# The opening of an adapter-and-mix kernel: first block of columns in two halves, two issuing queues, block 0 normalised first

## The reference

```python
# x: (8 samples, 1024 rows, 512), one row id of L0 and one of L1 per sample
w1, w2 = W1[ids0], W2[ids0]                     # 512x128 and 128x512 per sample
h = relu(x @ w1 + b1[ids0])
r = x + h @ w2 + b2[ids0]
n = (r - mean(r)) * rsqrt(var(r) + 1e-5) * gamma[ids0] + beta[ids0]
x1 = x + n
out = x1 + x1 @ W[ids1] + b[ids1]               # 512x512 per sample
```

## Time and profile before

| | |
|---|---|
| median of 3 runs | 309.87 us (309.72 to 310.06) |
| the profiled execution | 310.4 us, its span 308.6 us |
| TensorE busy | 301.1 us (98%) |
| VectorE, GpSimd, ScalarE busy | 225.7, 225.7, 212.0 us |
| granted TensorE clock | 1.00 throughout |
| moved by DMA | 65.13 MB, mean 211 GB/s |

### The profile page before, as it was taken

One profiled execution on the slowest core, in us unless ns is written; L12 is line 12 of the kernel. 1 busy time (PEld: TensorE's weight loads), 2 busy tenths in 40 slices (PEclk: granted clock), 3 DMA queues, 4 the chain that ended last, 5 costly groups with the idle time before them and its releaser, 6 DMA issues.

```text
span 308.6 us, 4770 instructions
## 1 busy us (share of the span) xinstructions
PE 301.1 (98%) x1406; PEld 242.4 (79%) x1406; DVE 225.7 (73%) x643; ACT 212.0 (69%) x382; POOL 225.7 (73%) x185
## 2 busy tenths in 40 slices
PE   8789999999999999999999999999999999999995
PEld 6335788888888888888888888888888888888884
DVE  0089968886969879596887969688795968889610
ACT  1139778885887859686696858968596874867431
POOL 0299966999599995999779995999959994631000
PEclk9999999999999999999999999999999999999999
DMA  6999994879766896878866897668867371111122
GB/s 184 331 374 365 363 288 162 226 229 324 227 165 190 254 271 198 221 206 250 261 172 209 218 314 244 133 194 264 292 183 208 133 276 34 70 68 70 70 102 102
DMA packets 40817, 65.13 MB, mean 211 GB/s; under 512 B 6101, under 2 KB 10197, under 8 KB 40790
## 3 DMA queue, kind: packets, MB, share of 16 engines
q1 hardware_dynamic: 40498, 64.29, 67.8%
q10 hardware_dynamic: 292, 0.52, 0.5%
HBM read 48.03 MB, written 16.78 MB: 210 GB/s over the span
## 4 chain that ended last, share of the span: by engine, by line
PE 90%; DVE 3%; DMA 2%; SPq 2%; issue 1%; POOL 0%; ACT 0%; DVEq 0%
PE out_ps L814 56%; PE down_ps L814 13%; PE h_ps L814 13%; PE turn_ps L876 9%; DMA xrow<-x_rows 2%; DVE y L520 1%; SPq L177 1%; DVE stats L525 1%; SPq L186 1%; DVE turn_ps L564 0%; DVE x1T_lo L571 0%; POOL xrow L723 0%; PE out_ps L876 0%; ACT out_sb L423 0%; SPq L209 0%
## 5 line engine op out<-in xcount | busy, mean ns | idle before, releaser
L814 PE MATMUL out_ps<-x1T_hi,w_hi 128*128 128x512 f32 x256 | 100.0, 391 | 0.0
L814 PE MATMUL out_ps<-x1T_hi,w_lo 128*128 128x512 f32 x256 | 99.7, 389 | 0.0
L723 POOL TENSOR_TENSOR xrow<-xrow,b_rows 128x512 f32<-128x512 f32 x64 | 82.3, 1292 | 11.9 <-DMA xrow<-x_rows 11.7
L814 PE MATMUL out_ps<-x1T_lo,w_hi 128*128 128x512 f32 x256 | 68.6, 390 | 0.0
L414 ACT ACTIVATE x1T_hi<-turn_ps,gamma_beta 128x512 fp32r<-128x512 f32 x62 | 41.9, 690 | 37.7 <-DVE turn_ps L564 37.7
L564 DVE SCALAR_TENSOR_TENSOR turn_ps<-turn_ps,gamma_beta,xT 128x512 f32<-128x512 f32 x62 | 44.0, 752 | 32.4 <-PE turn_ps L876 31.7
L405 ACT ACTIVATE y<-y,shift,rstd 128x512 f32<-128x512 f32 x64 | 52.0, 817 | 22.0 <-DVE shift L555 21.7
L728 POOL TENSOR_TENSOR xT_lo<-xT,xT_hi 128x512 fp32r<-128x512 f32 x48 | 62.2, 1296 | 1.5 <-ACT xT_hi L354 1.5
L520 DVE TENSOR_TENSOR y<-down_ps,xrow 128x512 f32<-128x512 f32 x64 | 43.7, 684 | 19.8 <-PE down_ps L814 18.8
L814 PEld LDWEIGHTS out_ps<-x1T_hi,w_hi 128*128 128x128 f32 x256 | 48.1, 188 | 10.2 <-ACT x1T_hi L414 0.2
L814 PEld LDWEIGHTS out_ps<-x1T_hi,w_lo 128*128 128x128 f32 x256 | 48.1, 188 | 9.9
(11 more groups left out here) (50 smaller groups left out, 359.6 us busy)
## 6 DMA issues: line engine op xcount, KB each, us to landing
out_cols<-out_sb SPq DMA_DIRECT2D x64, 256.0 KB, 2.8
xrow<-x_rows SPq DMA_DIRECT2D x30, 512.0 KB, 6.7
xT<-x_cols SPq DMA_DIRECT2D x28, 512.0 KB, 6.1
w<-w_all SPq DMA_DIRECT2D x8, 1024.0 KB, 7.6
w<-w_all SPq DMA_DIRECT2D x16, 256.0 KB, 5.2
b_rows<-b_all SPq DMA_DIRECT2D x7, 256.0 KB, 8.8
xT<-x_cols SPq DMA_DIRECT2D x6, 256.0 KB, 6.0
xrow<-x_rows SPq DMA_DIRECT2D x4, 256.0 KB, 6.7
```

The costliest lines, as they stand in the source:

```text
L723: nc.gpsimd.tensor_tensor(xrow[:, i % XR, :], xrow[:, i % XR, :], b2_rows[:, m % 2, :], ALU.add).then_inc(rowbias_done, 1)
L814: mm = nc.tensor.matmul(out, lhsT, rhs, start=first and n == 0, stop=last and n == len(terms) - 1)
```

## The change

Six things go together, all in the opening:

- Column tiles 0 to 3 are loaded in two halves of 256 rows, each half in two DMAs of two column tiles (`load_first_half`), all four from ScalarE. The up products of block 0 run half by half (`up_first(h)`, four products of 128x256), into two banks, and `relu_first(h)` makes half of `hT`. down 0 and 1 need the first relu only, down 2 and 3 the second.
- ScalarE also issues row tiles 0 and 1, between the two halves and behind its table activation. SyncE's list is reordered.
- b1 of sample 0 arrives as one row of 512 bytes behind b2 in the same zeroed tile, and a product of one column turns it (`spread_b1`).
- VectorE instead of GpSimd adds b2 to row tiles 0 and 1 (`first_bias_rows`).
- down 2 and 3 write the two `turn_ps` banks instead of `down_ps` (`summed_ps`), so down 2 to 5 wait for fewer additions.
- The lists are reordered: the statistics and norms of block 0 come earlier, turn 0 to 3 come before down 6 and 7 and up 11, and out_high(0) before up 14 and down 8. On ScalarE w_high(0, 0) and w_high(0, 1) stand before standard(1) and relu(1).

```diff
+        first_h_ps = [h_ps[0], out_ps[1]]
+        summed_ps = [turn_ps[i % 2] if 2 <= i < BLOCK else down_ps[i % 2] for i in range(TILES)]
+        def load_first_half(engine, h, c):
+            rows = slice(h * HALF, (h + 1) * HALF)
+            engine.dma_start(xT[:, 2 * c:2 * c + 2, rows],
+                             x_cols[2 * c * P:(2 * c + 2) * P, rows].rearrange("(k p) n -> p k n", p=P)
+                             ).then_inc(first_half_in[h][c], 16)
...
# SyncE
                 load_w1(0)
                 load_first_b2()
-                load_first_cols(sp, 2)
-                load_first_cols(sp, 3)
-                load_b1(0)
+                load_first_b1()
+                load_first_cols(sp, 4)
                 load_w2(0)
-                load_first_rows(0)
-                load_first_cols(sp, 4)
+                load_first_rows(sp, 2)
                 load_first_cols(sp, 5)
+                load_first_rows(sp, 3)
+                load_w(0)
                 load_first_cols(sp, 6)
-                load_first_rows(1)
-                load_first_rows(2)
-                load_first_rows(3)
+                load_first_cols(sp, 7)
                 load_rows(4)
-                load_first_cols(sp, 7)
-                load_w(0)
-                load_rows(6)
...
# ScalarE
-                load_first_cols(act, 0)
-                load_first_cols(act, 1)
+                load_first_half(act, 0, 0)
+                load_first_half(act, 0, 1)
                 load_ids()
                 load_table()
+                load_first_rows(act, 0)
+                load_first_rows(act, 1)
+                load_first_half(act, 1, 0)
+                load_first_half(act, 1, 1)
+                spread_b1()
                 spread_b2()
-                relu(0)
+                relu_first(0)
+                relu_first(1)
                 standard(0)
-                relu(1)
+                w_high(0, 0)
+                w_high(0, 1)
                 standard(1)
                 standard(2)
-                w_high(0, 0)
-                w_high(0, 1)
+                relu(1)
+                w_high(0, 2)
                 standard(3)
-                w_high(0, 2)
-                standard(4)
                 normalise(0)
                 normalise(1)
                 normalise(2)
+                standard(4)
                 normalise(3)
...
# VectorE
+                first_bias_rows(0)
+                first_bias_rows(1)
                 add_rows(0)
+                statistics(0)
+                mean_variance(0)
                 add_rows(1)
-                statistics(0)
+                rstd_start(0)
                 add_rows(2)
-                mean_variance(0)
-                rstd_start(0)
                 statistics(1)
+                statistics(2)
+                mean_variance(1)
                 rstd_newton(0)
...
# TensorE
+            def spread_b1():
+                pe.wait_ge(b1_first_in, 16)
+                product(turn_ps[0][:, 0:1], [(first_bias[:, D:D + P], ones[:, 0:1])]).then_inc(b1_product, 1)
+            def up_first(h):
+                rows = slice(h * HALF, (h + 1) * HALF)
+                for k in range(KC):
+                    if k % 2 == 0:
+                        pe.wait_ge(first_half_in[h][k // 2], 16)
+                    if h == 0 and k == 0:
+                        pe.wait_ge(w1_in[0], 16)
+                    mm = product(first_h_ps[h][:, rows], [(w1[:, 0, k], xT[:, k, rows])], first=k == 0, last=k == KC - 1)
+                mm.then_inc(half_up_done, 1)
...
-                up(0)
-                up(1)
+                up_first(0)
+                spread_b1()
                 spread_b2()
-                up(2)
-                up(3)
                 up(4)
+                up_first(1)
                 down(0)
                 down(1)
+                down(2)
                 up(5)
-                down(2)
+                down(3)
                 up(6)
-                down(3)
                 up(7)
                 down(4)
                 down(5)
-                down(6)
-                down(7)
                 up(8)
                 up(9)
                 up(10)
-                up(11)
                 turn(0)
                 turn(1)
                 turn(2)
                 turn(3)
+                down(6)
+                down(7)
+                up(11)
                 up(12)
                 up(13)
+                out_high(0)
+                out_low(0)
                 up(14)
-                up(15)
                 down(8)
-                out_high(0)
                 down(9)
```

More of the change, by code:

```diff
@@ L475, in opening @@
                 x1_high(7)
+                w_high(1, 0)
+                normalise(9)
                 standard(10)
-                normalise(8)
-                normalise(9)
             def step(s):
@@ L586, in opening @@
                 add_rows(3)
-                mean_variance(1)
+                rstd_start(1)
+                rstd_end(0)
+                rstd_start(2)
+                rstd_newton(1)
                 statistics(3)
-                rstd_start(1)
-                rstd_newton(1)
-                mean_variance(2)
-                add_rows(4)
[L593 to L605, removed]
+                rstd_newton(2)
+                rstd_end(1)
+                mean_variance(3)
+                mean_shift(0)
+                rstd_end(2)
+                add_rows(4)
                 mean_shift(1)
                 mean_shift(2)
+                statistics(4)
+                rstd_start(3)
@@ L608, in opening @@
+                mean_variance(4)
+                rstd_newton(3)
                 rstd_end(3)
                 mean_shift(3)
[L610 to L616, removed]
+                rstd_start(4)
+                add_rows(5)
+                rstd_newton(4)
                 merge(0)
                 merge(1)
-                rstd_start(5)
@@ L620, in opening @@
[L620 to L625, removed]
+                statistics(5)
+                merge(2)
+                x1_low(0)
+                merge(3)
+                x1_low(1)
+                rstd_end(4)
+                x1_low(2)
+                mean_variance(5)
+                mean_shift(4)
+                add_rows(6)
+                x1_low(3)
+                rstd_start(5)
@@ L626, in opening @@
+                statistics(6)
+                mean_variance(6)
+                add_rows(7)
+                statistics(7)
                 rstd_newton(5)
                 rstd_start(6)
-                x1_low(1)
-                mean_shift(4)
+                rstd_end(5)
+                mean_variance(7)
                 rstd_newton(6)
-                x1_low(2)
-                x1_low(3)
-                rstd_end(5)
+                rstd_end(6)
                 rstd_start(7)
+                rstd_newton(7)
@@ L635, in opening @@
+                mean_shift(5)
+                rstd_end(7)
                 add_rows(8)
-                rstd_end(6)
-                mean_shift(5)
+                mean_shift(6)
+                mean_shift(7)
                 statistics(8)
+                mean_variance(8)
                 add_rows(9)
[L640 to L645, removed]
                 merge(4)
@@ L647, in opening @@
                 merge(5)
+                rstd_start(8)
+                rstd_newton(8)
+                statistics(9)
                 x1_low(4)
+                x1_low(5)
+                mean_variance(9)
+                rstd_end(8)
+                mean_shift(8)
+                merge(6)
+                merge(7)
+                rstd_start(9)
                 add_rows(10)
+                rstd_newton(9)
                 statistics(10)
-                mean_variance(9)
-                rstd_start(8)
@@ L653, in opening @@
[L653 to L661, removed]
                 rstd_end(9)
+                mean_shift(9)
                 x1_low(6)
                 x1_low(7)
-                mean_shift(9)
+                mean_variance(10)
             def step(s):
@@ L861, in down @@
                     terms = [(hi, w2_hi[:, m % 2]), (hi, w2_lo[:, m % 2]), (lo, w2_hi[:, m % 2])]
-                product(down_ps[i % 2][:], terms).then_inc(down_done, 1)
+                product(summed_ps[i][:], terms).then_inc(down_done, 1)
             def turn(i):
@@ L867, in turn @@
                     pe.wait_ge(ident_done, 1)
-                if i == 3:
-                    pe.wait_ge(b2_spread, 1)
+                if 2 <= i < BLOCK:
+                    pe.wait_ge(y_done, i + 1)
                 if k == 0:
```

169 lines of the change are left out of this document (102 added, 67 removed).

## The result

The changed kernel took 312.22 us (median of 17 runs, 310.24 to 314.14), the kernel before 309.87 in its 17 runs beside them (309.22 to 310.41). The ratio is 1.008, 95% interval 1.0064 to 1.0095: 0.8% slower. The profiled execution took 311.75 us with a span of 310.0, against 308.6 before.

The account below looks back on a forecast made before the run. TensorE is full from 24.33 us, so only the opening matters. Down 0 at 14.6 plus VectorE's row puts turn 0 at 26.2 against 25.2: +1.0 us, median 310.9, range 308.5 to 312.5.

Parts of the forecast that it names:

- The yardstick: End of the opening: turn 0 starting at 25.19 us means no change, if no wait follows behind it.
- the draw: Start of turn 0 that leaves the time unchanged: 25.19 us, when 18 products were done in the kernel before.
- From down 0 to turn 0: VectorE's row of additions, statistics and norms, then normalise(3): turn 0 about 11.6 us after down 0, 14.6 to 26.2.
- Its own way through relu(1): TensorE's path by up 7, relu(1), down 4 and five products: turn 0 possible at 25.8, hidden by 0.4 us.
- The casts w_high: On ScalarE ahead of standard(1) and relu(1), waiting for W: hidden by 0.8 us, through relu(1) by 0.4.
- the issue of ScalarE's loads: Second half issued behind table activation and row tiles 0 and 1, at about 4.9 and 5.3 us, landing at 13.7.
- its own list of signs: Right: half 1 after 13 us, TensorE wait about 4 us, turn 0 near 26.2. Wrong: half 1 within 12.6 us.
- Rival 3: ScalarE's queue gets its four loads in early, half 1 before 12.5, W unchanged: +0.3 us, 310.2; chance 0.15.
- The clock: Clock falls to 1.2 GHz behind a TensorE wait of about 4 us before 13.7: +2.7 us, 312.6; chance 0.12.
- b1 by a product: Load queue of the opening: no 128 small pieces for b1, between 0 and 1.2 us saved, taken as 0.4.
- Rival 2: Queue runs fast from the start, the slow stretch being b1's small pieces: -1.6 us, 308.3; chance 0.25.
- The queue rule: Opening loads: spreading DMAs over issuing engines adds no bandwidth, so unit 10 or 11 stays so in landing order.

Follow-up runs that it names:

- e11: The changed kernel itself run again, beside e9 and e10: 313.23 us (6 runs), ratio 1.0092 to the kernel before.
- e1: Changed kernel with ScalarE waiting for its table activation before its four loads (row tiles 0 and 1, second half): 312.61 us, 1.0082 of the kernel before.
- e2: Changed kernel with 20 warm-up products instead of 10, loads untouched: 310.36 us, ratio 1.0015 to the kernel before.
- e3: Changed kernel with both edits, ScalarE's wait for its table activation and 20 warm-up products: 311.89 us, ratio 1.0061 to the kernel before.
- e5: As e1, but ScalarE issues the second half ahead of row tiles 0 and 1: 309.84 us, 0.9992 of the kernel before.
- e9: e5 with column tiles 6 and 7 issued before W, w_high(0, 0) and (0, 1) behind relu(1), 12 warm-up products: 309.26 us, 0.9977 of the kernel before.
- e7: e2 with w_high(0, 0) and w_high(0, 1) moved behind relu(1) on ScalarE: 311.41 us, ratio 1.0041 to the kernel before.
- e6: e2 with up 8 ahead of down 4 and the addition of tile 4 behind block 0's norms: 311.20 us, ratio 1.0036 to the kernel before.
- e8: The kernel before with only b1 of sample 0 arriving as one row and turned by a one-column product: 309.93 us, ratio 0.9999.
- e4: The kernel before with only row tiles 0 and 1 moved from SyncE's list to ScalarE's: 312.18 us, ratio 1.0063.
- e10: e9 with down 3 behind up 7 and the norms of tiles 0 to 2 ahead of tile 3's addition: 310.44 us, 1.0014 of the kernel before.

## Why the prediction was right in its number and wrong in its cause

Forecast: +1.0 us, 310.9, range 308.5 to 312.5. Measured: +1.4 us of span in the profiled pair, +2.35 us in the medians, slower as forecast and inside the range.

| kernel | down 0 | turn 0 | turn 0 less down 0 | span | span less turn 0 |
|---|---|---|---|---|---|
| forecast | 14.6 | 26.2 | 11.6 | 309.6 | |
| changed | 14.98 | 26.55 | 11.57 | 310.0 | 283.45 |
| e11, changed again | 16.74 | 28.31 | 11.57 | 311.7 | 283.4 |
| e1 | 14.90 | 26.47 | 11.57 | 309.9 | 283.4 |
| e2 | 14.04 | 25.60 | 11.56 | 309.0 | 283.4 |
| e3 | 14.80 | 26.36 | 11.56 | 309.7 | 283.3 |
| e5 | 12.66 | 25.42 | 12.76 | 308.8 | 283.4 |
| e9 | 11.81 | 24.84 | 13.03 | 308.2 | 283.4 |

- **The yardstick held.** Turn 0 was 1.36 us behind the draw, the span 1.4 us longer; in the seven profiles of the table the span less turn 0 is the same to 0.15 us, and the kernel before has the same 283.4 behind its draw (308.6 less 25.19). No wait of TensorE was left behind turn 0.
- **From down 0 to turn 0 held**, and for the reason given: 11.6 forecast, 11.57 in five profiles. VectorE's row, through ScalarE's last norm, sets turn 0. The norm ended at 26.40 and the weights of the first transpose were loaded from 26.52. TensorE's last product in front of it started its last pass at 25.90, so by its rhythm of 0.43 us a pass the engine was free at 26.33. Its own way through relu(1) was 0.2 us shorter, not 0.4. ScalarE and TensorE in the changed kernel:

```profile
25.59 0.81 ACT L440 ACTIVATE y<-y,shift,rstd 128x512 f32<-128x512 f32 x1
...
26.52 0.86 PEld L952 LDWEIGHTS out_ps<-ident,y 128*128 128x128 f32 x8 [0.86 <-issue]
```

  The same 0.15 us lies between the end of the norm and turn 0 in e1, e2, e5, e7, e9 and e11; in e6, where the norms were early, there is no gap behind the last product. The casts w_high were hidden, as stated, in the changed kernel, and no longer in e5, where down 0 was 2.3 us earlier.
- **The step that failed is the issue of ScalarE's loads.** "Behind its table activation ... at about 4.9 and 5.3 us" was read from program order. They were issued from 2.66 us. So the second half was early (10.1, forecast 13.7) and W1 was late (first product 7.83, forecast 5.8). By its own list of signs the prediction is wrong here: the half landed within 12.6 us, and the wait of about 4 us ahead of it did not come. e1 is the forecast's order, and there the half landed when it was said to, down 0 was at 14.90, and nothing was won. That down 0 lies within 0.4 us of the forecast in the changed kernel too is luck: another load and the clock made up the time. Without the clock's part it would be at about 13.3 (an estimate: 7.83, and the 5.47 us that e2 took from its first product to down 0).
- **Rival 3**, given 0.15, named the early issue and the early half (before 12.5), and priced it at +0.3 us. It left out what these loads take from W1, 2.07 us of the start, and the clock behind that.
- **The clock**, given 0.12 as a rival, is the second cause, behind another wait than the one named. Behind a wait of 2.19 us the granted clock was 0.64 from 8 to 11 us. It costs 1.7 us (changed kernel against e2, first product to up 4); that the prediction put down 1.7 us too, for two other products at 1.2 GHz, is chance. The Trainium skill (TensorE: Matmul & The Clock Gate, Part 1) has idle time take the array to 1.2 GHz; e2, whose fill kept the clock at 0.999 to 1.0 in all runs, agrees. The length of the wait alone does not tell it: e9 waited 2.02 us for relu(1), after 11 us of products without a wait, and its clock stayed at 1.00; and in e8 the first products were slow behind no wait. All slow first products (changed kernel, e4, e8, e11) came behind 10 warm-up products, and none behind the 20 of e2, e3, e6 and e7, by their profiles.
- **What evened it out.** From its first product to turn 0 the changed kernel lost 3.2 us (18.72 less 18 x 0.86) where the kernel before had lost 4.0 up to the same count. Of its 3.2 us the clock is 1.7, so that apart from the clock it lost 1.5 us, 2.4 less than before: the reordering did save time. The later start (2.07 us) and the clock (1.7) took more, and 1.4 us of loss are left. Without the clock, e2 comes to 1.0015.
- **b1 by a product**: put at 0.4 us of the queue; 0.5 for the next load, 0 for the time (e8). Rival 2, the fast queue, falls with it.
- **The queue rule.** The Trainium skill (DMA: Bandwidth & Descriptors, Rules for kernel authors) holds that a second issuing engine adds no bandwidth. The traces do not agree: from 8 to 11 us 302 GB/s were moved in e4, which differs from the kernel before only in where two loads are issued, and 379 in the changed kernel, against 248 before. So more was moved early on, and still TensorE started later: W1 was issued at 2.78 us in e4 and at 2.81 before, and beside two loads that nobody needed yet it held the first product up 2.15 us longer.

Still open: the upper runs of e1, whose profile was its second fastest execution, were never profiled, so that the clock's part in its median of 312.61 is only argued from the granted clocks listed. Why the first product comes anywhere from 7.83 to 9.22 us in kernels with the same order of the first loads (changed kernel, e2, e6, e7, e11) is not explained either.

## What to carry to other kernels

Where an opening is bound by its loads, as this one is, the order of issue over all queues is the schedule (e4, e5); write down when each issue really happens in the trace, since a load issue can run ahead of the compute that stands before it in the same list, and put the load that starts TensorE ahead of everything. A wait of TensorE near the start can cost twice, here 2.2 us as a wait and 1.7 us as products at half rate behind it; ten more dummy products were cheap against that (e2). Moving one wait away pays only up to the next: check what the filler itself needs (e6), and what the moved work uncovers behind it (e9, e10).

## What was not expected of the hardware

- ScalarE issued loads from 2.66 us while its table load (2.59, 1.28 us long) was running and the activation ahead of them in the list had not started (3.88). So the list of an engine gives the order of its instructions, but not that a load's issue waits until the activation before it has run. One wait on that activation restores the order (issues from 4.12 us in e1).
- Two additions of VectorE with two operands in SBUF took 2.37 us in the changed kernel, beside two of GpSimd that took 3.42. In e1, with GpSimd idle, the two took 1.29, and one of GpSimd alone 1.26. Timelines of VectorE and GpSimd in the changed kernel, then of VectorE in e1:

```profile
13.29 2.37 DVE L559 TENSOR_TENSOR xrow<-xrow,b_rows 128x512 f32<-128x512 f32 x2 [11.60 <-ACT b_rows L384]
```

```profile
13.36 3.42 POOL L775 TENSOR_TENSOR xrow<-xrow,b_rows 128x512 f32<-128x512 f32 x2 [11.88 <-ACT b_rows L384]
```

```profile
9.84 1.29 DVE L561 TENSOR_TENSOR xrow<-xrow,b_rows 128x512 f32<-128x512 f32 x2 [8.15 <-ACT b_rows L386]
```

  So the 0.61 us each that the prediction took for these additions holds only apart from GpSimd. The Trainium skill (GPSIMD Engine Reference, Specifications) says that GpSimd's SBUF interfaces are shared with VectorE, with contention when VectorE's instruction has two SBUF inputs; the trace agrees.
- The granted clock in the records can be 1.00 while products run at half rate: in e11 eight passes of 256 columns took 3.75 us in a window of clock 1.00, and 1.97 us in e2. The duration of products is the better witness. By it the warm-up products of e2 ran at half rate until about 6.3 us and those of e3 until about 4.6 (estimates from their counts by windows), though their records say 1.00 all along. Ten of them end at 5.4 to 5.7 us, so they can be over before the full rate has come. That this is what made the first products of e8 and e11 slow is not shown.
